# Causal attention with sixteen biased exponentials a step on ScalarE, in place of one subtraction on VectorE and one exponential

## The reference

```python
q, k = rope(h @ wq, h @ wk)          # 32 query heads, 8 key heads of 64
s = q @ k.T / sqrt(64) + causal      # per sequence and head, 64 x 64
p = softmax(s, axis=-1)              # exp(s - max) / sum
out = (p @ v) @ wo                   # four query heads share a key/value head
```

## Time and profile before

| what | value |
|---|---|
| median of 3 runs | 2600.49 us |
| span of the profiled execution | 2704.4 us |
| TensorE, VectorE, ScalarE, GpSimd busy | 83%, 68%, 43%, 41% of the span |
| mean granted clock of TensorE | 0.907 |

### The profile page before, as it was taken

How to read it: one execution, slowest core, us unless ns; L and a number is a source line. 1 busy time by engine, 2 the same in 40 slices (tenths; PEclk the granted TensorE clock), 3 DMA queues, 4 the chain that set the end, 5 groups by cost and what they waited for, 6 DMA issues and landing times. The chain is left out here.

```text
span 2704.4 us, 60407 instructions
## 1 busy us (share of the span) xinstructions
PE 2250.3 (83%) x20880; PEld 1699.7 (63%) x20880; DVE 1841.5 (68%) x3965; ACT 1152.8 (43%) x2509; POOL 1105.8 (41%) x1111
## 2 busy tenths in 40 slices
PE   6889989786878579994799899899888699998890
PEld 4555555443766357773677777787766577886670
DVE  4888888762547567775878878878876365444654
ACT  2777667554434223332344444444333354332230
POOL 2455555554144400001445445455577301325526
PEclk9898899765889689997999999999999799999995
DMA  5555455433358431211332332332334462445644
GB/s 115 125 134 141 121 137 131 113 114 100 104 178 277 133 130 52 64 31 51 82 83 62 81 85 59 81 87 57 85 100 135 134 206 90 142 148 167 200 153 144
DMA packets 249859, 313.10 MB, mean 116 GB/s; under 512 B 45152, under 2 KB 202848, under 8 KB 249056
## 3 DMA queue, kind: packets, MB, share of 16 engines
q1 hardware_dynamic: 188592, 219.11, 28.9%
q0 software_dynamic: 26624, 58.79, 7.9%
q10 hardware_dynamic: 34352, 31.34, 3.4%
HBM read 122.40 MB, written 102.24 MB: 83 GB/s over the span
## 5 line engine op out<-in xcount | busy, mean ns | idle before, releaser
L2119 POOL TENSOR_TENSOR ca_qk<-ca_qk,ca_q_swap 128x512 f32<-128x512 f32 x160 | 249.9, 1562 | 371.2 <-DVE ca_q_swap L2297 369.6
L735 DVE TENSOR_REDUCE soft_top<-soft_pa 128x2 fp32r<-128x512 f32 x512 | 328.4, 683 | 99.6 <-PE soft_pa L816 81.8
L630 ACT ACTIVATE soft_prob<-soft_pb 128x512 f32<-128x512 f32 x512 | 286.0, 594 | 191.8 <-PE soft_pb L809 171.9
L809 PE MATMUL soft_pb<-soft_rep 32*128 32x256 f32 x1024 | 213.4, 368 | 62.1 <-DVE soft_top L735 39.6
L809 PEld LDWEIGHTS soft_pb<-soft_rep 32*128 32x128 f32 x1024 | 140.1, 218 | 181.8 <-issue 85.8
L1440 PE MATMUL moe_pgu<-moe_w_hi,moe_xt_hi 128*128 x472 | 198.1, 420 | 39.8 <-DVE moe_xt_lo L1357 24.9
L816 PE MATMUL soft_pa<-soft_rep 31*128 31x256 f32 x1024 | 223.0, 375 | 6.0 <-DVE soft_top L735 3.5
L1459 PE MATMUL moe_py<-moe_w_d,moe_at 128*128 x788 | 219.1, 394 | 1.7 <-issue 0.8
L1363 DVE TENSOR_TENSOR moe_act_f<-moe_silu,moe_pgu 128x256 f32<-128x256 f32 (+1 forms) x236 | 88.5, 375 | 165.4 <-ACT moe_silu L1258 111.2
L2389 PE MATMUL ca_py<-ca_w_hi,ca_ot_hi 128*128 128x256 f32 x512 | 154.4, 302 | 33.1 <-DVE ca_ot_lo L2318 32.8
L1258 ACT ACTIVATE moe_silu<-moe_pgu 128x256 f32<-128x256 f32 (+1 forms) x236 | 82.1, 348 | 230.0 <-PE moe_pgu L1440 149.8
(11 more groups left out here) (377 smaller groups left out, 6384.7 us busy)
## 6 DMA issues: line engine op xcount, KB each, us to landing
ca_q_swap<-ca_q_f SPq DMA_DIRECT2D x640, 64.0 KB
moe_xs<-moe_rows SPq DMA_DIRECT2D x236, 128.0 KB
soft_rep<-soft_parts SPq DMA_DIRECT2D x378, 64.0 KB
moe_rows<-soft_blank SPq DMA_DIRECT2D x27, 768.0 KB
moe_ys_rows<-moe_ys ACTq DMA_DIRECT2D x134, 128.0 KB
moe_ys<-moe_ys ACTq DMA_DIRECT2D x102, 128.0 KB
moe_xd<-scratch SPq DMA_DIRECT2D x64, 128.0 KB
ca_vs<-ca_v SPq DMA_DIRECT2D x32, 256.0 KB
```

The costliest lines, as they stand in the source:

```text
L630: act.activation(prob[:, k % 4, h, :], p_b[:, 2 * T * h:2 * T * (h + 1)], ACT.Exp).then_inc(prob_ready, 1)
L735: dve.tensor_reduce(heads[:, j, :, g], p_a[:, 2 * T * h:2 * T * (h + 1)].rearrange("p (c s) -> p c s", c=HALF), AX, ALU.max).then_inc(a_do ...
L809: mm = pe.matmul(p_b[:, out], rep[of, i % 4, g, at:at + PART], rep[of, i % 4, g, 0:T], start=True, stop=True)
L2119: pool.tensor_tensor(qk[:, u % 2, m, :], qk[:, u % 2, m, :], q_swap[:, p % 2, :], ALU.add).then_inc(qk_ready, 1)
```

## The change

The exponential of a step is split in sixteen, one for each group of 64 columns: ScalarE reads the scores from PSUM and adds the negated maximum of the group as a per-partition bias. VectorE negates the maxima as it takes them, and no longer subtracts. ScalarE issues 3 of the 16 after the first turned half, 9 after the second, 4 after the last projection's copy. The sums and their reciprocals move from the middle of VectorE's step to its end. The scores of the next step now wait for the exponentials (`prob_ready`), not for the subtraction.

```diff
--- before.py
+++ after.py
@@ -1985,7 +1985,7 @@
         swapped = [sem(f"swap{i}") for i in range(2)]
         qk_ready, v_mm, v_ready = sem("qk"), sem("v_mm"), sem("v")
         vs_in = [sem(f"vs{i}") for i in range(2)]
-        s_ready, top_ready, sm_ready, prob_ready = sem("s"), sem("top"), sem("sm"), sem("prob")
+        s_ready, top_ready, prob_ready = sem("s"), sem("top"), sem("prob")
         sum_ready, rsum_ready, pn_ready = sem("sum"), sem("rsum"), sem("pn")
         pt_mm, pt_ready = sem("pt_mm"), sem("pt")
         pv_ready, othi_ready, otlo_ready = sem("pv"), sem("othi"), sem("otlo")
@@ -2172,6 +2172,18 @@
                         past(act, pv_ready, n)
                         act.activation(pt[:, t, :], p_t[:], ACT.Copy).then_inc(pt_ready, 1)
 
+                def exps(n, first, end):
+                    if not live(n):
+                        return
+                    if first == 0:
+                        act.wait_ge(top_ready, n + 1)
+                        past(act, pt_mm, 2 * (n - 1))
+                    for g in range(first, end):
+                        at = slice(g * SEQ, (g + 1) * SEQ)
+                        op = act.activation(sm[:, n % 2, at], p_s[:, at], ACT.Exp, bias=top[:, g:g + 1])
+                    if end == 16:
+                        op.then_inc(prob_ready, 1)
+
                 for n in steps:
                     now = projected(n)
                     if live(n - 2):
@@ -2184,9 +2196,7 @@
                     for u, m in now[0:1]:
                         fetch(u, m)
                     turned(n - 1, 0)
-                    if live(n):
-                        act.wait_ge(sm_ready, n + 1)
-                        act.activation(sm[:, n % 2, :], sm[:, n % 2, :], ACT.Exp).then_inc(prob_ready, 1)
+                    exps(n, 0, 3)
                     new = fresh(n, 4)
                     if new is not None:
                         act.wait_ge(rstd_ready, 2 * new + 2)
@@ -2198,8 +2208,10 @@
                     for u, m in now[1:2]:
                         fetch(u, m)
                     turned(n - 1, 1)
+                    exps(n, 3, 12)
                     for u, m in now[2:]:
                         fetch(u, m)
+                    exps(n, 12, 16)
                     ch, j = step_of(n)
                     if j < 2 and 0 <= ch < CHUNKS:
                         for t in (2 * j, 2 * j + 1):
@@ -2304,13 +2316,8 @@
                     groups = lambda a: a.rearrange("p (g k) -> p g k", k=SEQ)
                     if live(n):
                         dve.wait_ge(s_ready, n + 1)
-                        past(dve, sm_ready, n)
-                        dve.tensor_reduce(top[:], groups(p_s[:]), AX, ALU.max).then_inc(top_ready, 1)
-                        dve.wait_ge(top_ready, n + 1)
-                        past(dve, pt_mm, 2 * (n - 1))
-                        dve.tensor_tensor(groups(sm[:, n % 2, :]), groups(p_s[:]),
-                                          top[:].unsqueeze(2).to_broadcast([PART, 16, SEQ]), ALU.subtract
-                                          ).then_inc(sm_ready, 1)
+                        past(dve, prob_ready, n)
+                        dve.tensor_reduce(top[:], groups(p_s[:]), AX, ALU.max, negate=True).then_inc(top_ready, 1)
                     if live(n - 2):
                         for rho in range(2):
                             dve.wait_ge(othi_ready, 2 * (n - 2) + rho + 1)
@@ -2325,12 +2332,6 @@
                         rope(u, m, True)
                     for u, m in now[0:1]:
                         rope(u, m, False)
-                    if live(n):
-                        dve.wait_ge(prob_ready, n + 1)
-                        dve.tensor_reduce(sums[:], groups(sm[:, n % 2, :]), AX, ALU.add).then_inc(sum_ready, 1)
-                        dve.wait_ge(sum_ready, n + 1)
-                        past(dve, pn_ready, n)
-                        dve.reciprocal(rsum[:], sums[:]).then_inc(rsum_ready, 1)
                     for u, m in now[0:1]:
                         rope(u, m, True)
                     for u, m in now[1:2]:
@@ -2353,6 +2354,12 @@
                         rope(u, m, True)
                     for u, m in now[2:]:
                         rope(u, m, False)
+                    if live(n):
+                        dve.wait_ge(prob_ready, n + 1)
+                        dve.tensor_reduce(sums[:], groups(sm[:, n % 2, :]), AX, ALU.add).then_inc(sum_ready, 1)
+                        dve.wait_ge(sum_ready, n + 1)
+                        past(dve, pn_ready, n)
+                        dve.reciprocal(rsum[:], sums[:]).then_inc(rsum_ready, 1)
                     r = routing(n, 4)
                     if r is not None:
                         route.spread(dve, r, routed_row(r))
@@ -2429,7 +2436,7 @@
                     u, h = n // 2, n % 2
                     if h == 0:
                         pe.wait_ge(qk_ready, M5 * (u + 1))
-                    past(pe, sm_ready, n)
+                    past(pe, prob_ready, n)
                     for s in range(2):
                         half = slice(SEQ * s, SEQ * s + SEQ)
                         pe.matmul(p_s[:, s * CHUNK:(s + 1) * CHUNK].rearrange("p (g k) -> p g k", k=SEQ), twice_r[half, :],
```

## The result

The changed kernel takes 2647.6 us against 2601.5 us, a ratio of 1.018 with a 95% interval of 1.0157 to 1.0204: 46 us slower. The forecast was 2652 and 52 us slower.

A forecast was written before the change was run, and what follows sets the result against it. TensorE was taken to set the pace, VectorE close behind. Chunk terms of 2.9 us eight times (23), j=5 (13), sends (14) and the stage's end (2) gave +52 us, 2652 us; range 2598 to 2725.

The forecast's parts named there:

- The exponentials: ScalarE: sixteen short exponentials of 0.317 us each, starts 0.224 apart, adding 2.6 us of work a step.
- The score buffer: Next scores wait for exponential 16: +0.86 us at j=2 (j = step mod 8); values' copies +0.6 at j=0.
- The ring: Late sums, GpSimd's multiply and addition, SyncE's swap, VectorE's rotary operations: 10.2 us per step, free in steps of 11 to 12.
- Place 3: Step mod 8 = 3 (step 27): transposes 1.8 us late behind the multiply, 0.7 hidden, so +1.1.
- place 5: Step mod 8 = 5: ht_lo ends late behind sums and router's statistics; +2.4 us in five chunks, +0.6 in two.
- j=3 and j=4 ... I count nothing: Steps mod 8 = 3, 4: two GpSimd roots delay sums to 16.6 and 15.3 us; other end, 1.5 gained per chunk.
- the clock: TensorE's granted clock: cost left out; a reading below 0.95 in the stage would show the prediction wrong.
- the sends: From step 50, two of five indirect sends on GpSimd lengthen its queue cycle to 12.3 us: +1.0 for 14 steps.
- The waits for `ot_lo`: TensorE's output projection waits 30.7 us for late VectorE in 18 waits; none of it counted as returned.
- No overlap: Rival: exponentials start 0.317 us apart, even steps 1.1 longer, odd some 0.7: 2702 us; chance 0.13.
- Relief wins: Rival: VectorE's 78 us less give back the whole 30.7 us, only 12 us of costs remain: 2582 us; chance 0.08.
- VectorE held by GpSimd: Rival: GpSimd's additions hold VectorE's rotary operations up to 1.2 us each, 64 times 38 in all: 2690 us; chance 0.11.

The follow-up runs named there:

- Eight_exps: sums_ahead with eight exponentials of 128 columns in place of sixteen of 64: 2603.4 us, 1.0007 against the kernel before.
- split_six: sums_ahead with ht_lo ahead of the router's statistics and the sixteen exponentials issued 6, 6 and 4 instead of 3, 9 and 4: 2590.8 us, 0.9955.
- late_sums: The kernel before, with only the sums and reciprocals moved to the end of VectorE's step: 2665.3 us, 1.0233.
- sums_ahead: The changed kernel, with sums and reciprocals ahead of the output addition, statistics and later rotary operations in VectorE's step: 2615.7 us, 1.0035.
- three_swaps: The changed kernel with three buffers for the swapped halves (q_swap) instead of two: 2619.0 us, 1.0057.
- exps_early: The changed kernel with all sixteen exponentials where the long one stood and sums and reciprocals in their old place: 2642.3 us, 1.0153.
- late_ht: The changed kernel with ht_lo ahead of the router's statistics at place 4 (step mod 8) on VectorE: 2644.9 us, 1.0168.

## Why the prediction came out

- *Bound and cover.* Right: TensorE sets the pace and the change moved no engine past it. The loss is made of waits.
- *The exponentials.* Thirteen took 2.77 us: with 0.344 for one, (2.77 - 0.344) / 12 = 0.202 between starts, against the 0.224 taken. The score buffer cost 0.65 us at place 2 (forecast 0.86, where its own 10.43 less 9.62 gives 0.81) and 0.42 at place 0 (forecast 0.6). Eight_exps and split_six show that both hang on the length of the run.
- *The ring.* Shown by four runs: late_sums makes it without the exponentials, sums_ahead takes out what stood in it, three_swaps cuts a link, exps_early is without it. Place 3 grew by 1.57 (forecast 1.1), place 5 by 2.38 (forecast 2.4), place 6 by 0.1 (0.3). That place 5 fits so well is luck in part: the forecast's own 5.4 less 2.4 gives 3.0, nothing in it tells where 0.6 went, and the five steps grew by 1.1 to 3.9 us, two of them with a stretch of half clock in them.
- *The term that failed: "j=3 and j=4 ... I count nothing".* Place 4 grew by 1.70 us, 8.5 in five chunks. The transposes there waited for the multiply, up to 5.36 us. I took the sums of step 27 to end 16.6 us after its start; they ended 20.2 after it (1607.21 less 1587.03). Two links were too short. The addition of 1.56 us began at 1596.28 and the next only at 1599.06, as VectorE's rotary operations were running; and the swap took 5.6 us, from 1599.18 to 1604.79, not 3.9; together that is 2.9 of the 3.6 us. The base was off as well: the 15.26 us of step 28 are the longest place 4 of chunks 1 to 5 before, with 3.4 us at half clock in them (1643.3 to 1646.6); the others took 13.7 to 14.5. So the gain of 1.5 in each chunk, the prediction's other end, was not there to be had.
- *The cost left out: the clock.* The prediction put it at nothing, with a granted clock below 0.95 in the stage as a sign of being wrong. It read 0.96 over the stage, against 0.98 before, and still goes with some 12 us by the estimate above. So the waits by themselves cost less in steps 0 to 47 than the forecast had, about 24 us against 30.
- *The term that was too large: the sends.* 14 us forecast from step 50 on; from the start of step 50 to that of 63 the stage takes 178.3 us before and 178.3 after, with the score buffer and the ring in it. The forecast set a ring of 12.3 us against steps of about 11.4; these 13 steps take 13.7 on average in the kernel before already, so the ring had room. The additions there were behind the sends before as well. What makes these steps long wasn't looked into, and no run took the sends out.
- *The sum* was right in part by luck, because these cancel. In steps 0 to 47 I had some 30 us and 36.1 came, later some 22 and 2.8 came, all of it in step 48, ahead of the sends. The terms were also not additive: late_ht removes the one at place 5 and gains 2.2 us in the stage, not 13.
- *The waits for `ot_lo`.* I returned nothing for the 30.7 us; 25.5 of them went, but they went in late_sums as well (8.5 left), where the steps are longer for other reasons, and 17.9 were back in sums_ahead. They are hidden, not gained.
- *Rivals.* No overlap: refuted by the 0.202. Relief wins: refuted by the time. VectorE held by GpSimd: as a cost of every step refuted, since VectorE's rotary operations on `q_swap` took 820 ns on average and not the 904 of before, and GpSimd's additions 1542 and not 1562. In the ring it did cost, the other way round: the addition of 1596.28 took 2.8 us while VectorE went from one rotary operation to the next. The statement of the Trainium skill that the prediction quotes (SBUF — State Buffer, Terms) names no side, and the trace agrees with it in both directions.

## What to carry to other kernels

When an instruction is replaced by many, ask less what they add to their engine than where the consumer of the last one must now stand, and what is queued behind that consumer on each engine it passes. A result used late can stall a queue whose other items were early: look for a ring through the queues (here sums, multiply, addition, swap, rotary operation), sum it, and compare it with the step; every item in it counts in full once it is longer. A cover of a long wait by another makes terms non-additive, so after removing one wait measure again before trusting the next. And look at the granted clock behind each new wait of TensorE: a wait of 2.1 us made a step 1.9 us longer where the clock stayed, and 3.4 where it fell.

## What the runs showed of the hardware

Biased exponentials of 128x64 from PSUM take 305 to 444 ns each (median 344), longer than the 317 worked out, but start 202 ns apart in a run of thirteen: they overlap by 0.14 us, more than the 0.093 of the longer scaled copies. And VectorE can hold GpSimd as well as be held, for longer than one instruction: additions took at most 1828 ns before and up to 2822 after. That longest one, at 1596.28, overlaps three rotary operations that follow each other without a gap, of 0.68 us each, and ends 1.2 us after the last of them:

```profile
L2119 POOL TENSOR_TENSOR ca_qk<-ca_qk,ca_q_swap x160: 1263/1598/2822, 1220.8 to 2073.0; 128x512 f32<-128x512 f32 x160
```
